# First of four images: normalisation moved from the pixels into the projection weights, and its front reordered

## The chip, the cores and the metric

One core of a Trainium2 chip runs the whole program. The metric is device time in microseconds (us) of one execution. TensorE (PE) multiplies matrices and writes PSUM; VectorE (DVE), ScalarE (ACT) and GpSimd (POOL) work element by element; SyncE (SP) issues the DMAs. Each engine works through its own instructions in the order in which they are written, and waits on semaphores that the others raise.

## The reference, cut to what matters

The input holds 4 images of 256 channels and 32 x 32 pixels, in float32.

```
gn(v):  per group of 8 channels: (v - mean) / sqrt(var + 1e-5)
x = x + concat(hifi, lofi)                        # 128 channels each, of gn(x)
  hifi: q, k, v = xw @ h_qkv_w                    # 4 heads of 32, windows of 2x2 pixels
        softmax(q k / sqrt(32)) v @ h_proj_w + h_proj_b
  lofi: q = xh @ l_q_w                            # every pixel
        k, v = mean over each 2x2 window @ l_kv_w # 256 pooled places
        softmax(q k / sqrt(32)) v @ l_proj_w + l_proj_b
x = x + conv3x3(relu(y * mask(y))) + bias,  y = gn(x)
```

The mask of a channel is found from its centre of mass. gn before a projection is one scale and one bias per channel and image: `gn(x) = s*x + t`.

## The kernel before, in words

Channels lie on the 128 partitions, in two tiles (`KT = 2`). Nearly every product is made in three float32r parts (`split_mm`, L1118: high by high, high by low, low by high), so each operand has a high part (a rounded copy) and a low part (what the rounding left). The six projections have names by their columns in the weights: WQ, WK, WV (window attention), WLQ, WLK, WLV (pooled attention).

An image passes through a *front* (projections, maxima of the pooled scores, window scores and their softmax) and a *rest* (exponentials, values, output projections); the convolution of the image before fills TensorE's waits. Image 0 has no convolution beside it. Its front runs like this. VectorE takes the statistics (`first_moments`, L652), TensorE averages them over groups (`group_means`, L1168) and warms up with four products of 384 columns (`keep_warm`, L1156), VectorE turns the averages into scale and bias (`normalisation`, L685). ScalarE and VectorE then both normalise the image (L455, L1093), VectorE forms the low part (L709), pools 2x2 windows (`pooling`, L712) and splits the pooled tile. TensorE does the projections WLQ, pooled WLK and WLV, WQ, WK, WV (`front`, L1263). ScalarE copies the queries' high part out of PSUM (L511), VectorE forms the low part (L840); then SyncE copies both within SBUF into the stacked operand `qs`, and the keys into `ks` (`stack`, L275): twelve copies, the first six of which release the first score block (semaphore `stacked`). Eight blocks of pooled scores follow (L1335), and VectorE takes the maxima of each (L851). The maxima are turned by TensorE (L1352), split by VectorE and copied into two more rows of `qs` (`stack_maxima`, L298), after which `pooled_scores` (L1234) can run. Beside this GpSimd multiplies queries by keys for the four places of a window (`products`, L377), TensorE sums them over each head (`window_scores_of`, L1252), ScalarE copies the sums (L594), TensorE transposes them (L1363), and VectorE does the window softmax (`window_maxima`, L863). TensorE turns the weights back (`turned_weights`, L1391), ScalarE copies them to `p_w` (L611).

In the rest, TensorE spreads the window weights (`values`, L1398) and VectorE multiplies them with the window values: four products into `pv` (L989). TensorE's pooled scores 5 to 7 stand behind `values(2)` and `values(3)`, which wait for the first and second of these products (L1417 to L1421). When all eight score tiles are through the exponentials (L566), TensorE sums them (`by_head`, L1242), projects the outputs, and goes on to image 1.

The convolution weights are also split on the way: VectorE makes two low parts (`first_weights`, L824, operations of L343) and three sums of taps (`turned_taps`, L830).

The order is written out by hand in every engine's block. PSUM has four tiles of two banks: `slot0` to `slot2`, and `cps`. In this file's lists `slot<-ks,qs` is a score block, `slot<-qs,ks` pooled scores, `cps<-mask,cst` and `cps<-probs,cst` window scores.

Of the kernel before, what the change touches and what calls it, by code (L numbers as in the profile page):

```python
# [5 lines left out]
F32 = mybir.dt.float32  # L6
# [7 lines left out]
P = 128  # L14
# [41 lines left out]
LA_SLOT = (0, 1, 2, 0, 1, 2, 0, 1)  # L56
ST_SLOT = (0, 1, 0, 1, 1, 0, 2, 1)
# [26 lines left out]
WARM = (4, 1)  # L84


PAIR_AFTER = (4, 7)
# [6 lines left out]
def pooled_by(images):  # L94


    return min(images, 1) + max(images - 2, 0)
# [21 lines left out]
def build(nc, x, wqkv, whp, wlp, bh, bl, cw, cb, mw, filt, consts, selectors, out):  # L119
    with ExitStack() as ctx:  # L120
# [34 lines left out]
        pv = (q_w[:], k_w[:], xn[:, 0], xn[:, 1])  # L155
# [5 lines left out]
        raw = probs[:, 2:4].rearrange("p a b -> p (a b)")  # L161
# [12 lines left out]
        pool_t, pool_s = mask[:, :, 0:2 * G], mask[:, :, 2 * G:3 * G]  # L174

# [7 lines left out]
        idle = sb("idle", [P, 1])  # L183

# [7 lines left out]
        cw_in, c_in, cst_in = sem("cw_in"), sem("c_in"), sem("cst_in")  # L192
        w_in = [sem(f"w_in{i}") for i in range(len(PIECES))]
        w_high, w_low, w_pooled = sem("w_high"), sem("w_low"), sem("w_low_pooled")
# [40 lines left out]
        def means_at(b, i):  # L235

            return (slot[1] if i == 0 else slot[2] if b else cps)[:, 0]
# [15 lines left out]
        def _(sp):  # L253
# [68 lines left out]
            for k in range(KT):  # L322
                sp.dma_start(raw_cw[:, k].rearrange("p r d c -> p (r d c)"), cw[k]).then_inc(cw_in, 16)
            stack(0)
            load(1)
            load(2)
            stack_maxima(0)
# [8 lines left out]
        def projection_low(engine, cols):  # L336

            return engine.tensor_tensor(w_lo[:, :, cols], raw_w[:, :, cols], w_hi[:, :, cols].bitcast(F32),
                                        ALU.subtract)

# [4 lines left out]
        def product(b, j):  # L345

            return mask[:, j] if b == 0 and j < 2 else qk[:, j]
# [14 lines left out]
        def _(pool):  # L362
# [7 lines left out]
            def mask_sum(b, pooled):  # L370

                pool.wait_ge(mask_c, (b + 1) * N_MASK)
                pool.wait_ge(pool_c, pooled_by(pooled) * N_POOL)
# [3 lines left out]
            def products(b):  # L377

                for j in range(NW):
                    if b == 0 and j == 2:  # L380
                        pool.wait_ge(proj_pe, 5)
# [32 lines left out]
            def step(b, first, last):  # L414
# [4 lines left out]
                if b == 1:  # L419
                    mask_sum(0, 2)  # L420
                    pool.wait_ge(v_dve, KT)
                    pool.wait_ge(lv_pe, 1)
# [3 lines left out]
                else:  # L426
# [3 lines left out]
                    nc.gpsimd.tensor_tensor(pv[0], pv[0], pv[1], ALU.add).then_inc(pv_pool, 1)  # L430
# [4 lines left out]
            pool.wait_ge(w_high, 1)  # L435
            projection_low(nc.gpsimd, PIECES[0]).then_inc(w_low, 1)
# [1107 lines left out]
```

## Time and profile before

| | |
|---|---|
| runs | 345.47, 345.17, 348.8 us; median 345.47 us |
| profiled execution | 345.89 us, of which 343.6 us are from the first to the last instruction |
| busy | PE 311.3 us (91%), DVE 270.2 us (79%), ACT 148.5 us (43%), POOL 82.9 us (24%) |
| PE busy in slices of 8.6 us, tenths, first ten | 1 8 8 9 9 6 8 9 9 9 |
| granted PE clock in the same slices, tenths | 9 9 6 9 9 8 9 9 9 9 |

The busy rows say which engine works most; the slices show that the first 60 us are the emptiest. What bounds a stretch is read from its waits: a timeline row ends with the idle time before it and, after `<-`, what ended that idle time.

### The profile page before, as it was taken

How to read it: one execution, taken by the hardware profiler on the slowest of the kernel's cores; microseconds unless marked ns; L12 is line 12 of the kernel's file. 1: busy time of each engine (PE TensorE's matmuls, PEld its weight loads, DVE VectorE, ACT ScalarE, POOL GpSimd, SP SyncE). 2: the span in 40 equal slices, each digit the busy share in tenths (PEclk: the TensorE clock that was granted, in tenths of full speed). 3: DMA queues.
4: the chain of work that ended last, by engine and by line, in shares of the span. 5: the costliest groups of instructions: out<-in, count | busy, mean ns of one | idle time of the engine just before them, and what ended most of it. 6: DMA issues, size and time to landing. Idle time of an engine off the chain costs nothing.

```text
span 343.6 us, 4160 instructions
## 1 busy us (share of the span) xinstructions
PE 311.3 (91%) x1566; PEld 220.8 (64%) x1566; DVE 270.2 (79%) x488; ACT 148.5 (43%) x189; POOL 82.9 (24%) x46
## 2 busy tenths in 40 slices
PE   1889968999979899999799999999799999999995
PEld 1477444277966653788477645888487737877884
DVE  4973969878998696979989877789887757897572
ACT  2533549572672644453058854450255424031300
POOL 2084912440454020005900200009600200202000
PEclk9969989999989999999999999999999999999999
DMA  7789500029500000198011100396001000001003
GB/s 274 284 105 142 228 5 0 2 38 128 66 0 4 2 1 2 27 126 137 6 61 61 64 0 0 50 132 114 4 0 63 0 0 32 31 0 63 0 0 122
DMA packets 12067, 20.38 MB, mean 59 GB/s; under 512 B 2064, under 2 KB 8080, under 8 KB 11792
## 3 DMA queue, kind: packets, MB, share of 16 engines
q1 hardware_dynamic: 12048, 20.13, 28.5%
q8 instruction: 12, 0.20, 0.2%
q14 instruction: 7, 0.06, 0.1%
HBM read 7.93 MB, written 4.19 MB: 35 GB/s over the span
## 4 chain that ended last, share of the span: by engine, by line
PE 55%; DVE 25%; ACT 8%; issue 6%; POOL 3%; DMA 2%; SPq 0%; DVEq 0%; POOLq 0%
PE slot L1116 28%; PE cps L1148 15%; PE slot L1192 7%; DVE l_max L851 5%; DVE mask L787 3%; PE cps L1192 2%; ACT probs L566 2%; POOL probs L382 2%; DVE v_lo L817 1%; DMA xy<-x 1%; PE slot L1394 1%; PE cps L1116 1%; ACT xn_hi L455 1%; ACT p_w L611 1%; DVE xn L743 1%
## 5 line engine op out<-in xcount | busy, mean ns | idle before, releaser
L1148 PE MATMUL cps<-v_hi,cw_hi 128*128 128x512 f32 (+1 forms) x144 | 57.6, 400 | 3.6 <-DVE v_lo L817 2.9
L1148 PE MATMUL cps<-v_hi,cw_lo 128*128 128x512 f32 (+1 forms) x144 | 58.4, 405 | 0.0
L1148 PE MATMUL cps<-v_lo,cw_hi 128*128 128x512 f32 (+1 forms) x144 | 56.5, 392 | 0.0
L382 POOL TENSOR_TENSOR probs<-q_w,k_w 128x1024 f32<-128x1024 f32 x14 | 32.9, 2378 | 78.9 <-DVE rw L780 71.8
L851 DVE TENSOR_REDUCE l_max<-slot 128x4 f32<-128x1024 f32 x32 | 37.0, 1218 | 6.3 <-PE slot L1116 6.3
L566 ACT ACTIVATE probs<-slot 128x1024 f32<-128x1024 f32 x32 | 31.2, 1021 | 13.9 <-PE slot L1116 13.6
L1148 PEld LDWEIGHTS cps<-v_hi,cw_hi 128*128 128x128 f32 x144 | 27.4, 191 | 12.5 <-issue 5.3
L1148 PEld LDWEIGHTS cps<-v_hi,cw_lo 128*128 128x128 f32 x144 | 27.4, 190 | 9.0 <-issue 4.0
L1148 PEld LDWEIGHTS cps<-v_lo,cw_hi 128*128 128x128 f32 x144 | 27.4, 190 | 5.3 <-issue 0.4
L365 POOL TENSOR_TENSOR mask<-rw 128x1024 f32<-128x1024 f32 x8 | 15.2, 1910 | 56.2 <-DVE rw L780 56.2
L1116 PE MATMUL slot<-xn_hi,w_hi 128*128 128x512 f32 (+1 forms) x68 | 28.0, 412 | 0.8 <-DVE xn_lo L709 0.8
L1116 PE MATMUL slot<-xn_hi,w_lo 128*128 128x512 f32 (+1 forms) x68 | 26.7, 392 | 0.0
L1116 PE MATMUL slot<-xn_lo,w_hi 128*128 128x512 f32 (+1 forms) x68 | 26.6, 391 | 0.0
L549 ACT ACTIVATE xn<-mask 128x1024 f32<-128x1024 f32 x8 | 8.5, 1061 | 39.0 <-DVE mask L787 39.0
L560 ACT ACTIVATE v_hi<-mask 128x1024 fp32r<-128x1024 f32 x16 | 16.8, 1058 | 18.0 <-DVE mask L809 10.6
L1116 PE MATMUL slot<-qs,ks 98*128 98x512 f32 x64 | 20.8, 419 | 2.0 <-DMA qs<-probs 2.0
L817 DVE SCALAR_TENSOR_TENSOR v_lo<-mask,v_hi 128x1024 fp32r<-128x1024 f32 x16 | 19.2, 1221 | 3.8 <-ACT v_hi L560 3.8
L1116 PE MATMUL slot<-probs,cst 128*32 128x512 f32 x176 | 21.4, 596 | 0.0
L1116 PEld LDWEIGHTS slot<-ks,qs 96*128 96x128 f32 x128 | 18.2, 194 | 4.3 <-DVE l_max L851 2.1
L430 POOL TENSOR_TENSOR q_w<-q_w,k_w 128x1024 f32<-128x1024 f32 x3 | 7.2, 2415 | 56.8 <-DVE k_w L989 56.8
L1116 PE MATMUL slot<-ks,qs 96*128 96x256 f32 x128 | 19.6, 290 | 1.2 <-DVE l_max L851 0.8
L535 ACT ACTIVATE xn<-xy,gn 128x1024 f32<-128x1024 f32 x8 | 9.6, 1240 | 17.2 <-DVE gn L682 17.2
(197 smaller groups left out, 627.7 us busy)
## 6 DMA issues: line engine op xcount, KB each, us to landing
xy<-x SPq DMA_DIRECT2D x8, 512.0 KB, 5.9
out<-xy SPq DMA_DIRECT2D x8, 512.0 KB, 2.6
qs<-probs SPq DMA_DIRECT2D x12, 256.0 KB, 5.8
qs<-probs SPq DMA_DIRECT2D x24, 128.0 KB, 8.2
raw_cw<-conv_w SPq DMA_DIRECT2D x2, 1152.0 KB, 7.2
ks<-probs SPq DMA_DIRECT2D x12, 128.0 KB, 6.9
probs<-h_qkv SPq DMA_DIRECT2D x2, 192.0 KB, 4.3
probs<-l_kv SPq DMA_DIRECT2D x2, 128.0 KB, 4.3
```

The costliest lines, as they stand in the source:

```text
L365: nc.gpsimd.tensor_tensor(mask[:, k].rearrange("p (h w) -> p h w", h=H), rw[:, k, 0].unsqueeze(2).to_broadcast([P, H, W]), rw[:, k, 1].uns ...
L382: nc.gpsimd.tensor_tensor(product(b, j).rearrange("p (n w) -> p n w", n=NW), q_w[:].rearrange("p (n w) -> p n w", n=NW), k_w[:, j * G:(j + ...
L535: nc.scalar.activation(xn[:, k], img(b, k), ACT.Identity, bias=gn[1][:, 6, k:k + 1], scale=gn[1][:, 5, k:k + 1]).then_inc(yn_ready, 1)
L549: nc.scalar.activation(xn[:, k], mask[:, k], ACT.Relu).then_inc(relu, 1)
L560: nc.scalar.activation(v_hi[:, k, 2 * phase:2 * phase + 2].rearrange("p a b -> p (a b)"), mask[:, k], ACT.Copy, scale=TILE_SCALE[phase]).t ...
L566: nc.scalar.activation(probs[:, i], flat[score_slot(b, i)], ACT.Exp, scale=SCALE / NW)\
L787: nc.vector.scalar_tensor_tensor(mask[:, k], mask[:, k], -1.0, xn[:, k], ALU.max, ALU.mult).then_inc(masked, 1)
L817: nc.vector.scalar_tensor_tensor(v_lo[:, k, part].rearrange("p a b -> p (a b)"), mask[:, k], TILE_SCALE[phase], v_hi[:, k, part].rearrange ...
L851: nc.vector.tensor_reduce(l_max[:, bass.ds(n, HEADS, step=NB)], flat[LA_SLOT[n]].rearrange("p (h m) -> p h m", h=HEADS), AX_X, ALU.max, ne ...
L1116: return nc.tensor.matmul(dst, lhsT, rhs, start=start, stop=stop)
L1148: ins = nc.tensor.matmul(cps[:, pos % 2, y0 * WT:y1 * WT], (cw_hi, cw_hi, cw_lo)[part][:, k, pos, dy + 1, o * P:(o + 1) * P], (v_hi, v_lo, ...
L1192: ins = nc.tensor.matmul(last_bank(o, pos)[:, y0 * WT:y1 * WT], (cw_hi, cw_hi, cw_lo)[part][:, k, pos, dy + 1, o * P:(o + 1) * P], (v_hi, ...
```

## The change

For image 0 alone, the scale is multiplied into the projection weights instead of the pixels, and the bias becomes a shift of each projection's result (a product of the raw weights with the bias, added when a result is copied out of PSUM; the shifts of the values are carried into the output bias). The raw image is split into high and low part, the high one while the statistics run. The pooled keys and values are no longer projected from a pooled tile but summed by TensorE over the four places of a window (24 products of 256 columns for the keys, 48 of 128 columns for the values, where there were 6 and 12). Afterwards the plain weights are split again for the images 1 to 3. The raw weights now lie in the place of image 2, whose load therefore comes later. The front of image 0 has an order of its own on each engine; the normalisation of image 1 moves forward on VectorE, in front of the convolution weights. The diff, cut to its core:

```diff
-WARM = (4, 1)
-PAIR_AFTER = (4, 7)
+WARM = (3, 1)
+LA_SLOT_0 = (0, 1) * 4
+FIRST_KEYS, FIRST_VALUES = (4, 4, 4, 0, 0, 0, 0, 0), (0, 0, 0, 4, 4, 4, 0, 0)
...
+            load_taps(1)
             stack(0)
             load(1)
+            load_taps(0)
+            stack_maxima(0)
+            sp.wait_ge(w_high, len(PIECES) + 1)
...
             load(2)
-            stack_maxima(0)
...
             def inner_weights():
                 t = taps[1]
+                pool.wait_ge(gn_c[0], 2 * N_GN)
                 link(nc.gpsimd.tensor_tensor(t[:, 0], t[:, 0], t[:, 2], ALU.add), 5)
...
+            def first_step():
+                input_high()
+                scaled_weights()
+                first_projections()
...
+                input_moments(1, 0)
+                act.wait_ge(lv_pe, 1)
+                values_of(slot[2])
...
+                plain_weights()
+                act.wait_ge(ssum_pe, 1)
+                nc.scalar.copy(q_w[:], flat_cps).then_inc(ssum_sb, 1)
+                act.wait_ge(cw_in[0], 16)
+                weight_high(0, V_LEFT, 0)
+                weight_high(0, V_RIGHT, 2)
...
+            def first_front():
+                normalisation(0, 0)
+                dve.wait_ge(gn_c[0], N_GN)
+                input_low(0)
+                scaled_weights(0)
+                input_low(1)
+                scaled_weights(1)
+                scaled_weights(2)
+                query_lo(0)
+                key_lo(0)
+                dve.wait_ge(zeroed, 1)
+                maxima(0, range(NB))
+                maxima_parts(0)
...
+                plain_weights()
+                first_bias()
...
+                window_maxima(0)()
+                normalisation(1, 0)
+                first_weights(weights)
+                turned_taps(weights)
...
+                pe.wait_ge(shift_act, 2)
+                keys, vals = Projection(cps, WK), Projection(slot[2], WV)
+                for n in range(NB):
+                    keys.more(FIRST_KEYS[n])
+                    if n == NB - NW - 1:
+                        pe.wait_ge(qkv_sb, 1)
+                    vals.more(FIRST_VALUES[n])
+                    if n == 0:
+                        pe.wait_ge(stacked, STACK)
+                        pe.wait_ge(lq_dve, 1)
+                    elif n == 1:
+                        pe.wait_ge(lk_act, 1)
+                        pe.wait_ge(lk_dve, 1)
+                    else:
+                        pe.wait_ge(la_max, n - 1)
...
+                    for h in range(HEADS):
+                        ins = mm(flat[LA_SLOT_0[n]][:, h * G:(h + 1) * G], qs[0:SC, h, n * P:(n + 1) * P], ks[0:SC, h],
+                                 True, True)
+                    ins.then_inc(la_pe, 1)
+                pe.wait_ge(qkv_sb, 3)
+                pe.wait_ge(w_in[1], KT * 16)
+                shift_of(WV, slot[2][:, 1, AT_SHIFT + S_V:AT_SHIFT + S_V + 1])
+                shift_of(WLV, slot[2][:, 1, AT_SHIFT + S_LV:AT_SHIFT + S_LV + 1])
+                values_of_sums(slot[2])
+                window_scores_of(0, (0, 1), cps)
+                pe.wait_ge(zeroed, 1)
+                pe.wait_ge(la_max, NB)
+                nc.tensor.transpose(slot[2][:, 0, 0:P], l_max[:], cst[:, C_ID:C_ID + P]).then_inc(lmt_pe, 1)
+                window_scores_of(0, (2, 3), cps)
```

TensorE, from the projection of the window values to the turn of the maxima, before (`cps<-xn_hi,w_lo` is the last product of that projection):

```order
L1116 MATMUL cps<-xn_hi,w_lo 128x512
L1116 MATMUL slot<-ks,qs 128x256 [waits qkv_sb,stacked]
L1116 MATMUL slot<-ks,qs 128x256 [waits lk_dve,lk_act]
L1116 MATMUL slot<-ks,qs 128x256 [waits la_max]
L1116 MATMUL slot<-ks,qs 128x256 [waits third_stacked,la_max]
L1116 MATMUL cps<-mask,cst 32x512 [waits prod_ready,qkv_sb]
L1116 MATMUL slot<-ks,qs 128x256 [waits fourth_stacked,la_max]
L1116 MATMUL cps<-probs,cst 32x512 [waits prod_ready,qkv_sb]
L1352 MATMUL slot<-cst,l_max 128x128 [waits la_max,zeroed]
```

The same place now (the key projection `cps<-xn_hi,w_hi` and value projection `slot<-xn_hi,w_hi` stand between the score blocks; `slot<-w_hi,xn_hi` is the first of the 48 products of the pooled values):

```order
L1233 MATMUL cps<-xn_hi,w_hi 128x512 [waits shift_act]
L1233 MATMUL slot<-ks,qs 128x256 [waits lq_dve,stacked]
L1233 MATMUL cps<-xn_lo,w_hi 128x512 x4
L1233 MATMUL slot<-ks,qs 128x256 [waits lk_dve,lk_act]
L1233 MATMUL slot<-xn_hi,w_hi 128x512 [waits qkv_sb]
L1233 MATMUL slot<-ks,qs 128x256 [waits fourth_stacked,la_max]
L1233 MATMUL slot<-gn,xy 128x1 [waits w_in1,qkv_sb]
L1233 MATMUL slot<-w_hi,xn_hi 128x128
L1233 MATMUL cps<-mask,cst 32x512 [waits prod_ready] x2
L1468 MATMUL slot<-cst,l_max 128x128 [waits la_max,zeroed]
L1233 MATMUL cps<-xn,cst 32x512 [waits prod_ready] x2
```

Eight products of the keys and all twelve of the values came ahead of the first score block and now stand behind its wait; the pooled values and both pairs of window scores follow the last block.

VectorE, from the end of the window softmax to the first product with the window values, before:

```order
L878 CAST k_w<-k_w 128x32x4 [waits soft_c]
L879 TENSOR_TENSOR k_w<-k_w 128x32x4 [waits soft_c]
L833 TENSOR_TENSOR raw_cw<-raw_cw 128x3x256
L834 TENSOR_TENSOR raw_cw<-raw_cw 128x3x256 [waits cw_dve]
L835 TENSOR_TENSOR raw_cw<-raw_cw 128x3x256 [waits cw_dve]
L989 TENSOR_TENSOR q_w<-slot,v_w 128x1024 [waits pb_pe]
```

The same place now (between L777 and L763 stand ten more small instructions of the normalisation of image 1):

```order
L994 TENSOR_TENSOR k_w<-k_w 128x32x4 [waits soft_c]
L777 COPY gn<-slot 128x4 [waits gn1_pe]
L763 SCALAR_TENSOR_TENSOR gn<-gn 128x2 [waits gn1_c]
L355 TENSOR_TENSOR cw_lo<-raw_cw,cw_hi 128x768 [waits cw_act]
L355 TENSOR_TENSOR cw_lo<-raw_cw,cw_hi 128x768 [waits cw_dve]
L943 TENSOR_TENSOR raw_cw<-raw_cw 128x3x256 [waits cw_dve]
L944 TENSOR_TENSOR raw_cw<-raw_cw 128x3x256 [waits cw_dve]
L945 TENSOR_TENSOR raw_cw<-raw_cw 128x3x256 [waits cw_dve]
L1127 TENSOR_TENSOR q_w<-slot,v_w 128x1024 [waits pb_pe]
```

The twelve instructions of the normalisation and the two low parts of convolution weights now stand between the softmax and the first window product; before, the low parts came ahead of the maxima and the normalisation after the window products.

## Rows read from the trace of the kernel before

**Rows 1.** The page's first line: span of the profiled execution.

```profile
span 343.6 us, 4160 instructions
```

**Rows 2.** TensorE's timeline: start, duration, line, operation, count, idle before it.

```profile
7.68 0.56 PE L1116 MATMUL slot<-mv,cst 128*128 128x4 f32 x2 [7.68 <-DVE mv L664]
8.11 5.04 PE L1116 MATMUL cps<-cst 128*128 128x384 f32 x8
...
14.49 0.39 PE L1116 MATMUL slot<-xn_hi,w_lo 128*128 128x512 f32 x1
14.72 0.39 PE L1116 MATMUL slot<-xn_hi,w_hi 128*128 128x512 f32 x1
...
18.89 0.48 PE L1116 MATMUL slot<-p_w,w_hi 128*128 128x256 f32 x2 [1.91 <-DVE w_lo L338]
```

**Rows 3.** SyncE's timeline: issues of the copies into the stacked operands, images 0 and 1.

```profile
18.05 2.39 SPq L278 DMA_DIRECT2D qs<-probs  x3
22.97 1.84 SPq L282 DMA_DIRECT2D ks<-probs  x3
...
74.55 1.93 SPq L278 DMA_DIRECT2D qs<-probs  x3
```

**Rows 4.** DMA issues at 24.3 to 24.8 us: KB, us to landing (image 0's sixth copy).

```profile
ks<-probs SPq DMA_DIRECT2D x1, 128.0 KB, 5.2
```

**Rows 5.** TensorE's timeline: score blocks, window scores, pooled scores, image 1's first block.

```profile
32.56 1.60 PE L1116 MATMUL slot<-ks,qs 96*128 96x256 f32 x12
...
36.40 1.91 PE L1116 MATMUL cps<-mask,cst 128*32 128x512 f32 x8
...
39.85 2.62 PE L1116 MATMUL cps<-probs,cst 128*32 128x512 f32 x8
...
46.63 1.97 PE L1116 MATMUL slot<-qs,ks 98*128 98x512 f32 x4 [1.96 <-DMA qs<-probs]
...
85.87 2.06 PE L1116 MATMUL slot<-ks,qs 96*128 96x256 f32 x12 [0.26 <-DMA ks<-probs]
```

**Rows 6.** Stretches: length, busy us by engine (PE, PEld, DVE, ACT, POOL), PE clock, DMA, GB/s.

```profile
12.60:16.00 3.40, 2.60 (x11) 1.73 (x10) 3.34 (x4) 1.74 (x3) 0.00 (x0) 1.00 0.97 407
19.40:26.20 6.80, 6.80 (x25) 6.01 (x24) 4.73 (x6) 0.75 (x3) 6.72 (x5) 0.50 1.10 141
46.70:50.10 3.40, 3.40 (x13) 2.91 (x13) 3.26 (x6) 1.94 (x2) 0.00 (x0) 0.50 0.01 2
70.00:343.60 273.60, 257.90 (x1327) 188.01 (x1325) 219.36 (x405) 112.41 (x143) 54.22 (x25) 0.99 0.23 42
87.76:93.07 5.31, 5.31 (x51) 5.31 (x49) 5.31 (x6) 2.24 (x4) 3.05 (x2) 1.00 0.50 58
```

**Rows 7.** Timelines of ScalarE and GpSimd: the queries' high part, a sum of taps.

```profile
17.02 1.01 ACT L511 CAST probs<-slot 128x1024 fp32r<-128x1024 f32 x1 [2.67 <-PE slot L1116]
...
40.48 1.80 POOL L404 TENSOR_TENSOR raw_cw<-raw_cw 128x768 f32<-128x768 f32 x1
```

**Rows 8.** VectorE's timeline, image 0, and image 1's normalisation.

```profile
23.60 3.70 DVE L343 TENSOR_TENSOR cw_lo<-raw_cw,cw_hi 128x768 fp32r<-128x768 f32 x2
33.31 9.19 DVE L851 TENSOR_REDUCE l_max<-slot 128x4 f32<-128x1024 f32 x8 [6.01 <-PE slot L1116]
...
47.15 0.29 DVE L879 TENSOR_TENSOR k_w<-k_w 128x128 f32<-128x128 f32 x1
...
49.33 0.96 DVE L835 TENSOR_TENSOR raw_cw<-raw_cw 128x768 f32<-128x768 f32 x1
...
52.16 1.22 DVE L989 TENSOR_TENSOR q_w<-slot,v_w 128x1024 f32<-128x1024 f32 x1 [1.86 <-PE slot L1116]
...
60.38 0.16 DVE L696 COPY gn<-slot 128x4 f32<-128x4 f32 x1
...
62.53 0.16 DVE L682 SCALAR_TENSOR_TENSOR gn<-gn 128x2 f32<-128x2 f32 x1
```

**Rows 9.** Chain of waits that ended last: start, us, what.

```profile
57.85 9.46 PE slot L1116 x70
```

More of the change, by code:

```diff
@@ L593, in step @@
                 act.wait_ge(ssum_pe, b + 1)
-                nc.scalar.copy(q_w[:], flat_cps if first else flat[0]).then_inc(ssum_sb, 1)
+                nc.scalar.copy(q_w[:], flat[0]).then_inc(ssum_sb, 1)
                 if b > 1:
@@ L900, in residual @@
                 dve.wait_ge(out_pe, b * 2 + k + 1)
-                last = nc.vector.scalar_tensor_tensor(img(b, k), flat[s], bias[:, k:k + 1], img(b, k), ALU.add, ALU.add)
+                if b == 0:
+                    dve.wait_ge(bias_first, 1)
+                add = bias[:, k:k + 1] if b else shift[:, S_OUT + k:S_OUT + k + 1]
+                last = nc.vector.scalar_tensor_tensor(img(b, k), flat[s], add, img(b, k), ALU.add, ALU.add)
                 last.then_inc(y_ready, 1)
@@ L1005, in step @@
                     conv_result(0, (V_LEFT,))
-                if not last:
+                if not last and not first:
                     normalisation(b + 1, 0)
@@ L1261, in window_scores_of, with __init__, more @@
                     ins.then_inc(ssum_pe, 1)
-            def front(b, conv, first=False):
+            class Projection:
+                def __init__(self, to, c0):
+                    self.to, self.c0, self.at = to, c0, 0
+                def more(self, n):
+                    for m in range(self.at, self.at + n):
+                        part, k, i = m // 4, m // 2 % 2, m % 2
+                        ins = mm(self.to[:, i], (w_hi, w_hi, w_lo)[part][:, k, self.c0:self.c0 + P],
+                                 (xn_hi, xn_lo, xn_hi)[part][:, k, halves(i)], m < 2, m >= 10)
+                        if m == 11:
+                            ins.then_inc(proj_pe, 1)
+                    self.at += n
@@ new lines, in shift_of, with first_keys @@
+            def shift_of(c0, to):
+                for k in range(KT):
+                    ins = mm(to, raw_w[:, k, c0:c0 + P], gn[0][:, 6, k:k + 1], k == 0, k == KT - 1)
+                return ins
+            def first_keys(parts):
+                for part in parts:
+                    for j in range(NW):
+                        for k in range(KT):
+                            ins = mm(slot[1][:, 0, 0:G], (w_hi, w_hi, w_lo)[part][:, k, WLK:WLK + P],
+                                     (xn_hi, xn_lo, xn_hi)[part][:, k, j * G:(j + 1) * G], part == j == k == 0,
+                                     part == 2 and j == NW - 1 and k == KT - 1)
+                return ins
@@ L1265, in front @@
+            def front(b, conv):
                 starting = b == 1
@@ L1374, in front @@
                     conv.more(EARLY)
-                elif not first:
+                else:
                     Convolution(b - 1).more(EARLY)
@@ L1455, in rest @@
                     window_out()
-                else:
+                elif not first:
                     group_means(b + 1, 0)
@@ L1488, in _ @@
             keep_warm(WARM[0])
[L1489 to L1492 removed]
+            first_front()
             run(step)
```

388 lines of the change are left out of this document (227 added, 161 removed).

## The prediction, made before the changed kernel was run

> **What bounds the kernel now.** I read the page first: its span is 343.6 us [rows 1]; with what lies around it the profiled execution took 345.89, 0.42 above the median of the runs, 345.47. All sums below are made against 345.89. Next the chain of waits: from 57.85 one unbroken piece of TensorE runs 9.46 us to the end of image 0's sums [rows 9]. So what matters ahead of it is when that piece may start, and the timelines give it backwards. Its last operands are exponentials whose scores 5 to 7 stand behind `values(2)` and `values(3)`, and those wait for VectorE's window products. The first of these starts at 52.16 [rows 8]. From there to 57.85 are 5.69 us. I take this distance over and ask when the first window product starts now; this is the hinge of the whole forecast.
>
> Before, three things lead up to it: the maxima (33.31, eight in 9.19, one each 1.15) [rows 8], the window scores (last pair ends at 39.85 + 2.62 = 42.47) [rows 5], and the softmax that follows these and ends at 47.15 + 0.29 = 47.44 [rows 8], 4.97 later. VectorE then makes sums of taps until 49.33 + 0.96 = 50.29 and sits idle 1.86 [rows 8].
>
> **Step 1: the start.** The warm-up has three products instead of four: it ends three quarters into its 5.04 us, at 8.11 + 3.7, near 11.9 [rows 2]. I give a shift (two products of one column, each two records) 0.4 from the two records of 0.2 at 7.68 to 8.11 [rows 2]. Then WLQ, twelve products of 512 columns at 14.72 - 14.49 = 0.23 [rows 2], with eight key products of 256 columns in between, each 0.12 (twelve in 1.60, less a tail of some 0.2) [rows 5]: 3.8 us, done near 16.6. The raw split, scaled weights and low parts are short operations on ScalarE and VectorE beside this stream, which start with the statistics or with the image; if the stream had to wait for one of them, everything below would be later by it. ScalarE copies the high part (1.01, before from 17.02 on [rows 7]) until 17.8, where the first stacked copy is issued; before it was 18.05 [rows 3]. Almost nothing is won here.
>
> **Step 2: the copies.** Before, the first of the six was issued at 18.05, the sixth at the end of its group, near 24.2 [rows 3], and landed 5.2 later [rows 4], at 29.4: 11.35 after the first. For image 1 the first was issued at 74.55 [rows 3] and TensorE, waiting for a key copy, started at 85.87 [rows 5]: 11.3 again. So the first block can start at 17.8 + 11.3 = 29.1. Before, TensorE reached it at 32.56 [rows 5], busy with projections: the wait was covered. Now it has, after 16.6, sixteen key products (1.9), a shift (0.4), WQ (2.8) and the first four products of WK (0.9): it is dry at 22.6 and stands still for 6.5 us. Eight products of WK and twelve of WV, ready all this time, are queued behind the wait.
>
> **Step 3: from the first block to the window scores.** Work in TensorE's queue at full clock: eight blocks of four at 0.12 (3.8), twenty products at 0.23 (4.7), two shifts (1.0), 48 products of 128 columns (5.3, [rows 6], 87.76 to 93.07), two pairs of window scores at 1.9 [rows 5], the turn of the maxima (0.2): 18.9. To this come 0.9 in which the last two blocks wait for maxima at 1.15 each, and the clock. After an idle 1.91 us [rows 2] the granted clock was 0.50, the lower of the two levels (1.2 and 2.4 GHz), from 19.4 to 26.2 [rows 6]; after 1.96 [rows 5] it was 0.50 from 46.7 to 50.1 [rows 6]. An idle 6.5 should do the same. Bounds for its cost: nothing if it stays up, 3.4 if it takes as long as the longer stretch; I take 2.5, between the 1.7 of the short stretch and the 3.4. The last pair ends at 29.1 + 18.9 + 0.9 + 2.5 = 51.4, against 42.47. Adding 4.97 the softmax ends at 56.4, against 47.44: **9.0 later**. GpSimd's four products can start when the keys are copied, near 35.5, and the second pair of scores needs the last of them near 49.5, so they hide if one takes under 3.5 (before, the second pair of scores followed the first by 39.85 - 36.40 = 3.45 [rows 5] with two products to wait for); so do the plain weights, split on ScalarE and VectorE while TensorE sums the values. Without their cover, two operations of 1536 columns would stand ahead of the softmax.
>
> **Step 4: VectorE after the softmax.** It now runs image 1's normalisation (60.38 to 62.53 + 0.16, 2.3), two low parts and the sums of taps (2.9 from 47.44 to 50.29) before the first window product. The low parts took 3.70 before [rows 8]. Their bounds: two operations of the size of a sum of taps, 1.9, and 3.7 as measured, when GpSimd worked at the same time. GpSimd's first sum of taps (1.80, [rows 7]) is now released by the same normalisation that frees VectorE, so they meet again; I take 3.7. The Trainium skill, SBUF — State Buffer, Who interferes with whom, says that a VectorE instruction with two SBUF inputs and a GpSimd one that reads SBUF exclude each other; by it the pair would cost 1.9 + 1.80, the same 3.7. Sum 9.0 with the gaps: the product starts at 56.4 + 9.0 = 65.4, against 52.16: **13.2 later**. The old idle 1.86 is gone, and the normalisation's old place, covered by TensorE's piece, gives nothing back.
>
> **Step 5: to the end of image 0.** The window weights are ready long before VectorE is, so TensorE idles about 5 us more ahead of `values(2)`. At the lower level the two values and two score tiles on the way cost double: I add 1.4, bounds 0 and 3.1 (another 1.7 if the long piece begins low too). One group mean, 0.3, leaves the piece at 57.85. Sum: 13.2 + 1.4 - 0.3 = 14.3, so **360.2 us**. From image 1 on the order is the old one, so the delay is carried to the end. The later load of image 2, the convolution weights on ScalarE, and GpSimd's share I cost at nothing: the image is needed a front later, the others are needed by the first convolution; if they came late, that would add.
>
> **Rivals.**
> - *The tail on VectorE is hidden.* If step 4 and 5 cost nothing (the low parts fit before the window weights come), only the 9.0 of the softmax counts: 345.89 + 9.0 - 0.3 = 354.6. For it: before, VectorE idled 1.86 there. Against: 9.0 of work stands in line where 4.7 was free.
> - *The copies land when TensorE gets there.* If copies within SBUF ran at the 407 GB/s of the weights' load [rows 6] instead of the 141 seen while they run, 1152 KB would take 2.8 and land near 23.1. No long wait, no low clock: last pair at 23.1 + 18.9 + 0.9 = 42.9, product at 42.9 + 4.97 + 9.0 = 56.9, 4.7 late: 350.3. Two images' copies with 11.3 speak against it. The Trainium skill, DMA: Bandwidth & Descriptors, Where 436 GB/s comes from, has the fabric's 435 as the limit for copies within SBUF; the trace does not agree, 141 is what moves.
> - *The delay is taken up behind.* TensorE is idle 273.6 - 257.9 = 15.7 us from 70 on [rows 6]. Were nearly all of that waits for things that image 0 does not delay, such as loads, the end would not move, and the shorter piece would leave 345.6: no slower. It decides from 14.3 of the 15.7. Against it: the late waits are for VectorE's and ScalarE's work on the images themselves.
> - *The early part wins and little is lost.* If TensorE reordered around the blocked score block, the last pair could come near 42 and only step 4 remain, about 350.
>
> **How the numbers follow.** Forecast 72%; hidden tail 12%; fast copies or reordering 6%; taken up behind 6%; something that makes it faster that I do not see 4%. The forecast's own range: 355 (clock stays up, low parts uncontended) to 364.5 (clock low through the blocks and the long piece). Taking in the hidden tail the range is 353.5 to 364.5. A change of 1% (3.5 us) is about what a measurement of this kernel can tell from none. Faster by over 1%: 0.04; within 1%: 0.06; slower by over 1%: 0.90.
>
> **What would show it.** The sixth copy's landing near 29 and TensorE's idle time before the first score block, ended by a DMA (step 2); a granted 0.50 after it; the 48 products between the last block and the window scores, and the softmax's end near 56 (step 3); two L343-like operations of together 3.7 and the first window product near 65, with no idle time of VectorE before it (step 4). Copies landing before 23, window scores done by 43, or VectorE idle before its first window product would make it wrong.

## The result and the profile after

The changed kernel takes 364.38 us (median; its four executions took from 363.0 to 365.93), the kernel before 345.32: a ratio of 1.0528, 95% interval 1.0442 to 1.0615. Slower, as forecast, and inside the range (353.5 to 364.5), but only 0.12 below its upper end: two of the four executions (365.61 and 365.93) lie above it, and the central 360.2 was 4.2 too low. A ratio leaves out executions over 1.5% above the fastest of their kernel, a median takes in all. The profiled execution took 365.93; its page's first line, against [rows 1]:

```profile
span 364.0 us, 4316 instructions
```

TensorE's timeline of the changed kernel (columns as in [rows 2]) answers to [rows 5]:

```profile
12.68 2.41 PE L1233 MATMUL slot<-xn_hi,w_hi 128*128 128x512 f32 x12
...
21.96 1.10 PE L1233 MATMUL cps<-xn_hi,w_hi 128*128 128x512 f32 x4
29.60 1.22 PE L1233 MATMUL slot<-ks,qs 96*128 96x256 f32 x4 [6.54 <-DMA ks<-probs]
...
40.58 0.74 PE L1233 MATMUL slot<-ks,qs 96*128 96x256 f32 x4 [0.67 <-DVE l_max L966]
41.15 0.95 PE L1233 MATMUL slot<-gn,xy 128*128 128x1 f32 x8
41.96 0.31 PE L1233 MATMUL slot<-w_hi,xn_hi 128*128 128x128 f32 x1
...
50.52 3.63 PE L1233 MATMUL cps<-mask,cst 128*32 128x512 f32 x8
...
54.40 1.91 PE L1233 MATMUL cps<-xn,cst 128*32 128x512 f32 x8
...
71.15 1.22 PE L1233 MATMUL slot<-p_w,sel 128*128 128x512 f32 x2 [5.34 <-DVE q_w L1127]
...
77.02 3.64 PE L1233 MATMUL slot<-probs,cst 128*32 128x512 f32 x32 [1.65 <-ACT probs L627]
```

Five things are to be seen. TensorE stands still 6.54 before the first score block, for a copy. The eight products of one column at 41.15 are the shifts of the values; behind them the 48 products of the pooled values run from 41.96 to 50.5, which is 8.5 for work that took 5.31 in [rows 6]. The first pair of window scores takes 3.63, the second 1.91. Before the third value product TensorE waits 5.34 for VectorE. And the sums start at 77.02; before, they started at 58.13, behind the group mean at 57.85 that opened the long piece [rows 9]:

```profile
58.13 3.64 PE L1116 MATMUL slot<-probs,cst 128*32 128x512 f32 x32
```

Stretches of the changed kernel's trace (columns as in [rows 6]; the clock is third from the right):

```profile
29.60:34.00 4.40, 4.40 (x15) 3.87 (x16) 1.80 (x2) 0.00 (x0) 0.00 (x0) 0.53 1.20 141
...
41.00:44.00 3.00, 3.00 (x29) 3.00 (x28) 1.78 (x2) 2.91 (x5) 3.00 (x2) 1.00 0.01 3
44.00:50.50 6.50, 6.50 (x32) 6.40 (x31) 0.00 (x0) 0.20 (x2) 1.15 (x1) 0.50 0.00 0
50.50:54.00 3.50, 3.50 (x9) 0.56 (x8) 0.00 (x0) 1.80 (x3) 0.00 (x0) 0.50 0.00 0
...
71.00:75.50 4.50, 4.21 (x10) 2.97 (x10) 3.80 (x5) 1.59 (x2) 2.71 (x2) 0.59 0.00 0
...
187.00:191.00 4.00, 3.78 (x15) 2.21 (x19) 3.44 (x5) 0.00 (x0) 3.77 (x3) 0.57 0.15 27
262.50:266.00 3.50, 3.50 (x17) 1.42 (x19) 1.93 (x3) 0.00 (x0) 2.86 (x2) 0.52 0.04 9
```

The lower level of the clock (0.50) holds from 44.0 to 54.0. It also holds for most of the stretches from 29.6, 71.0, 187 and 262.5 on. VectorE's timeline, from the end of the softmax to the first window product, answers to [rows 8]; GpSimd's timeline has a sum of taps beside it:

```profile
61.08 0.29 DVE L994 TENSOR_TENSOR k_w<-k_w 128x128 f32<-128x128 f32 x1
...
63.45 0.16 DVE L763 SCALAR_TENSOR_TENSOR gn<-gn 128x2 f32<-128x2 f32 x1
63.52 3.46 DVE L355 TENSOR_TENSOR cw_lo<-raw_cw,cw_hi 128x768 fp32r<-128x768 f32 x2
67.02 0.96 DVE L943 TENSOR_TENSOR raw_cw<-raw_cw 128x768 f32<-128x768 f32 x1
...
69.88 1.22 DVE L1127 TENSOR_TENSOR q_w<-slot,v_w 128x1024 f32<-128x1024 f32 x1
```

```profile
63.69 2.48 POOL L431 TENSOR_TENSOR raw_cw<-raw_cw 128x768 f32<-128x768 f32 x1 [18.54 <-DVE gn L763]
```

No idle time stands ahead of the first window product any more (1.86 in [rows 8]): VectorE is the one that is late.

### The profile page after: what moved, and what is told of

The parts are those of the page before. It is cut to its first block, busy times and chain, and to the rows that moved or that the text cites. A ratio compares the mean times of both kernels' runs of the same rounds, so it can differ in the third digit from the quotient of the medians.

```text
span 364.0 us, 4316 instructions
## 1 busy us (share of the span) xinstructions
PE 324.1 (89%) x1638; PEld 232.6 (64%) x1638; DVE 267.5 (74%) x489; ACT 150.4 (41%) x196; POOL 80.1 (22%) x44
## 4 chain that ended last, share of the span: by engine, by line
PE 61%; DVE 23%; ACT 6%; issue 5%; DMA 3%; SPq 1%; DVEq 0%
PE slot L1233 30%; PE cps L1265 16%; PE slot L1309 7%; DVE l_max L966 5%; PE cps L1233 4%; ACT probs L627 2%; PE cps L1309 2%; DMA ks<-probs 2%; DVE v_lo L927 1%; DVE mask L897 1%; DVE cw_lo L355 1%; DMA xy<-x 1%; DVE xy L1007 1%; DVE xn L853 1%; DVE st L739 1%
## 5 line engine op out<-in xcount | busy, mean ns | idle before, releaser
L1265 PE MATMUL cps<-v_hi,cw_hi 128*128 128x512 f32 (+1 forms) x144 | 58.6, 407 | 3.6 <-DVE v_lo L927 2.9
L1265 PE MATMUL cps<-v_hi,cw_lo 128*128 128x512 f32 (+1 forms) x144 | 59.3, 412 | 0.0
L1265 PE MATMUL cps<-v_lo,cw_hi 128*128 128x512 f32 (+1 forms) x144 | 57.4, 399 | 0.0
L408 POOL TENSOR_TENSOR probs<-q_w,k_w 128x1024 f32<-128x1024 f32 x12 | 28.2, 2384 | 78.9 <-DVE rw L890 71.8
L1233 PE MATMUL slot<-ks,qs 96*128 96x256 f32 x128 | 20.7, 295 | 7.6 <-DMA ks<-probs 6.8
L1233 PE MATMUL slot<-xn_hi,w_hi 128*128 128x512 f32 (+1 forms) x76 | 27.1, 393 | 0.0
L1233 PEld LDWEIGHTS slot<-ks,qs 96*128 96x128 f32 x128 | 19.1, 198 | 10.6 <-DMA ks<-probs 7.7
L1233 PE MATMUL slot<-xn_hi,w_lo 128*128 128x512 f32 (+1 forms) x76 | 25.7, 372 | 0.0
L1233 PE MATMUL slot<-xn_lo,w_hi 128*128 128x512 f32 (+1 forms) x76 | 25.4, 370 | 0.0
L621 ACT ACTIVATE v_hi<-mask 128x1024 fp32r<-128x1024 f32 x16 | 16.8, 1059 | 18.0 <-DVE mask L919 10.6
L1233 PE MATMUL slot<-probs,cst 128*32 128x512 f32 x176 | 22.5, 623 | 1.6 <-ACT probs L627 1.6
```

Of the source, the lines that this page charges most:

```text
L408: nc.gpsimd.tensor_tensor(product(b, j).rearrange("p (n w) -> p n w", n=NW), q_w[:].rearrange("p (n w) -> p n w", n=NW), k_w[:, j * G:(j + ...
L621: nc.scalar.activation(v_hi[:, k, 2 * phase:2 * phase + 2].rearrange("p a b -> p (a b)"), mask[:, k], ACT.Copy, scale=TILE_SCALE[phase]).t ...
L1233: return nc.tensor.matmul(dst, lhsT, rhs, start=start, stop=stop)
L1265: ins = nc.tensor.matmul(cps[:, pos % 2, y0 * WT:y1 * WT], (cw_hi, cw_hi, cw_lo)[part][:, k, pos, dy + 1, o * P:(o + 1) * P], (v_hi, v_lo, ...
```

## The experiments

Each was run beside the kernel before on its own chip, so ratios are compared, not microseconds; 0.01 is 3.5 us, and an expected time divided by 345.32 is an expected ratio. Positions come from each run's profiled execution. Edits are to the changed kernel, and experiment 3 holds those of 2.

**1. VectorE's tail off the path.**

```diff
                 input_moments(1, 0)
+                act.wait_ge(cw_in[0], 16)
+                weight_high(0, V_LEFT, 0)
+                weight_high(0, V_RIGHT, 2)
...
                 maxima(0, range(NB))
+                first_weights(weights)
+                turned_taps(weights)
                 maxima_parts(0)
...
                 normalisation(1, 0)
-                first_weights(weights)
-                turned_taps(weights)
```

> Moves one part: ScalarE's two high parts of convolution weights go ahead of its copy of the pooled values, VectorE's two low parts and three sums of taps go between the maxima and their split, where VectorE is idle 11.7 us. Image 1's normalisation stays behind the window softmax. Theory (step 4, this work stands on the path): the first window product starts near 64.4 instead of 69.9, TensorE's idle 5.3 us before the third value product are gone and with them its low clock after it: 357.5 to 359. Rival (the tail is covered by something else that ends as late): 363 to 364.4.

Measured: 358.64, ratio 1.0312 (1.0246 to 1.0379). VectorE's and TensorE's timelines:

```profile
45.28 1.95 DVE L355 TENSOR_TENSOR cw_lo<-raw_cw,cw_hi 128x768 fp32r<-128x768 f32 x2 [2.90 <-ACT cw_hi L549]
...
60.76 0.29 DVE L994 TENSOR_TENSOR k_w<-k_w 128x128 f32<-128x128 f32 x1
...
64.14 1.23 DVE L1127 TENSOR_TENSOR q_w<-slot,v_w 128x1024 f32<-128x1024 f32 x1 [0.86 <-PE slot L1233]
```

```profile
69.88 3.64 PE L1233 MATMUL slot<-probs,cst 128*32 128x512 f32 x32 [1.40 <-ACT probs L627]
```

The first window product starts 5.74 earlier, of which 0.32 is an earlier end of the softmax (61.05), and waits for TensorE again; the sums start 7.14 earlier. The normalisation, left in place, is hidden by the turn and copy of the window weights.

**2. The 48 products into the wait for the copies.**

```diff
+                shift_of(WV, slot[1][:, 1, AT_SHIFT + S_V:AT_SHIFT + S_V + 1])
+                shift_of(WLV, slot[1][:, 1, AT_SHIFT + S_LV:AT_SHIFT + S_LV + 1]).then_inc(shift_pe, 1)
+                values_of_sums(slot[1])
                 pe.wait_ge(shift_act, 2)
                 keys, vals = Projection(cps, WK), Projection(slot[2], WV)
...
-                shift_of(WV, slot[2][:, 1, AT_SHIFT + S_V:AT_SHIFT + S_V + 1])
-                shift_of(WLV, slot[2][:, 1, AT_SHIFT + S_LV:AT_SHIFT + S_LV + 1])
-                values_of_sums(slot[2])
```

> Moves the 48 products of the pooled values, with their shifts, into TensorE's wait for the stacked copies (into another bank). Theory (steps 2 and 3: TensorE stands idle 6.5 us with this work ready behind): the idle time before the first block falls under 1 us, the low clock after it is gone, the window scores end near 44 instead of 56.3, where GpSimd's products, started when the keys are copied near 33.5, end last (43.3): 352. If the 48 narrow products themselves lower the clock: it falls there too, from about 25 on, and the time is 355 to 357. Rival (the wait for the copies only becomes another wait, for maxima or copies): 360 or more.

Measured: 354.25, ratio 1.0168 (1.0105 to 1.0232). The timeline of TensorE, and the stretch of the 48 products:

```profile
29.43 0.74 PE L1233 MATMUL slot<-ks,qs 96*128 96x256 f32 x4 [0.30 <-DMA ks<-probs]
...
43.15 1.90 PE L1233 MATMUL cps<-xn,cst 128*32 128x512 f32 x6 [0.81 <-POOL xn L408]
```

```profile
22.60:28.00 5.40, 5.40 (x51) 5.40 (x50) 0.00 (x0) 0.50 (x1) 0.00 (x0) 1.00 1.14 130
```

The window scores end at 45.05 instead of 56.31, 11.3 earlier, and GpSimd's products end last, as expected. Here the 48 products do not lower the clock by themselves.

**3. Both**, with image 0's convolution weights loaded at the start and split in the same wait.

```diff
             load_taps(1)
+            load_taps(0)
             stack(0)
             load(1)
-            load_taps(0)
...
                 key_lo(0)
+                first_weights(weights)
+                turned_taps(weights)
                 dve.wait_ge(zeroed, 1)
```

> Both parts at once: the 48 products and their shifts in the wait for the stacked copies, and image 0's convolution weights off the path. Their load is issued at the start, ScalarE's high parts follow the queries' copy, VectorE's low parts and sums of taps lie in its wait for the first score block. Image 1's normalisation stays behind the window softmax. Theory (these two and the clock that they cost are the whole loss): softmax end near 50.1 as with the moved products alone, first window product 2.5 to 3.2 later (near 53), the long piece of sums near 59, against 58.13 before: 0.3% to 0.8% slower than before, with the two later stretches of low clock. Rival (a further 5 us or more of the loss lies elsewhere, in the copies or in the order of image 0's projections): the piece starts at 63 or later, over 1.5% slower.

Measured: 348.59, ratio 1.0018 (0.9987 to 1.0048): no difference from before that these runs can tell. VectorE's and TensorE's timelines:

```profile
54.49 1.23 DVE L1127 TENSOR_TENSOR q_w<-slot,v_w 128x1024 f32<-128x1024 f32 x1 [1.88 <-PE slot L1233]
```

```profile
60.23 3.64 PE L1233 MATMUL slot<-probs,cst 128*32 128x512 f32 x32 [1.40 <-ACT probs L633]
```

The sums start at 60.23, 16.8 earlier than in the changed kernel. A short low stretch (0.57 from 50.5 to 54.5) slowed TensorE ahead of the first window product, which came at 54.49 instead of 53. So these two places, with the clock that they cost, are 16.8 of the 18.9 by which the sums came late; the 2.1 that are left in this trace would be 0.6%, where the interval of the ratio ends at 0.48%.

**4. Keys and values ahead of the first block.**

```diff
-FIRST_KEYS, FIRST_VALUES = (4, 4, 4, 0, 0, 0, 0, 0), (0, 0, 0, 4, 4, 4, 0, 0)
+FIRST_KEYS, FIRST_VALUES = (12, 0, 0, 0, 0, 0, 0, 0), (12, 0, 0, 0, 0, 0, 0, 0)
```

> Undoes one part of the change: all twelve products of the keys and all twelve of the values stand ahead of the first score block again, the rest of the changed kernel stays. Theory (they were queued behind the wait for the stacked copies, steps 2 and 3): the idle 6.5 us before the first block fall to about 2; the blocks then follow the maxima, 1.23 each, and the last block ends near 39.6 instead of 41.2. If the clock still falls during the 48 products of the pooled values, the gain is only these 1.6: 362.8. If it stays up, another 5: 357.8. Rival (the blocks wait for the maxima anyway, the interleaving costs nothing): 364.4, unchanged.

Measured: 366.04, ratio 1.0537 (1.0454 to 1.0621): no gain that can be told. TensorE's timeline and two stretches:

```profile
29.46 1.65 PE L1233 MATMUL slot<-ks,qs 96*128 96x256 f32 x8 [1.86 <-DMA ks<-probs]
...
36.73 2.35 PE L1233 MATMUL slot<-ks,qs 96*128 96x256 f32 x8 [0.19 <-DVE l_max L966]
...
54.44 1.91 PE L1233 MATMUL cps<-xn,cst 128*32 128x512 f32 x8
```

```profile
37.00:40.00 3.00, 3.00 (x14) 2.79 (x15) 2.82 (x3) 2.76 (x7) 0.00 (x0) 0.50 0.83 343
...
44.00:46.00 2.00, 2.00 (x11) 2.00 (x11) 0.00 (x0) 0.00 (x0) 0.00 (x0) 0.50 0.00 0
```

The wait fell to 1.86, and the last block ended at 39.08 instead of 41.32, 2.2 earlier (1.6 expected). But the clock fell at 30.0, half a microsecond behind this wait of 1.86, as it did behind those of 1.91 and 1.96 in [rows 2] and [rows 5], and it stayed low until 53.9, through the blocks and all 48 products: the window scores end at 56.35. In the changed kernel it came back at 33.8, among key products. So the products between the blocks may be worth the clock, which neither theory had; no run varies this alone.

**5. What makes the clock fall at 44.** First the eight one-column products alone are moved into the wait, out of the place just ahead of the 48.

```diff
+                shift_of(WV, slot[1][:, 1, AT_SHIFT + S_V:AT_SHIFT + S_V + 1])
+                shift_of(WLV, slot[1][:, 1, AT_SHIFT + S_LV:AT_SHIFT + S_LV + 1]).then_inc(shift_pe, 1)
                 pe.wait_ge(shift_act, 2)
...
-                shift_of(WV, slot[2][:, 1, AT_SHIFT + S_V:AT_SHIFT + S_V + 1])
-                shift_of(WLV, slot[2][:, 1, AT_SHIFT + S_LV:AT_SHIFT + S_LV + 1])
                 values_of_sums(slot[2])
```

> Moves only the eight products of one column (the shifts of the values) from just ahead of the 48 products of the pooled values into TensorE's wait for the stacked copies. Theory 1 of the clock (the thin stretch of one-column products and the short wait just ahead made the clock fall at 44): the 48 products and the window scores run at granted 1.00, 0.8 + 5.0 us less: 358.6. Theory 2 (the 48 products themselves, or something earlier, make it fall): it falls again within the 48 products and only 0.8 is gained: 363.6.

Measured: 362.2, ratio 1.0401 (1.0339 to 1.0462).

```profile
40.60:46.20 5.60, 5.60 (x52) 5.55 (x50) 1.85 (x2) 3.17 (x6) 4.22 (x2) 1.00 0.00 2
...
57.60:66.00 8.40, 4.73 (x10) 3.31 (x11) 8.26 (x7) 2.93 (x3) 4.46 (x3) 0.50 0.00 0
```

The 48 products keep 1.00, and the window scores end at 48.32 + 1.91 = 50.23, 6.1 earlier: theory 1, whose 358.6 is a ratio of 1.0385. A part is given back: the clock falls at 57.2 instead and is low through the values and into the long piece. Then the same with eight such products also left ahead of the 48:

```diff
+                for c0, at in ((WV, S_V), (WLV, S_LV)):
+                    shift_of(c0, slot[2][:, 1, AT_SHIFT + at:AT_SHIFT + at + 1])
                 values_of_sums(slot[2])
```

> Control for the clock: as the run that moved the eight one-column products into the wait for the copies, but eight one-column products (the same ones again, their results unused) also stand just ahead of the 48 products of the pooled values. Theory 1 (this thin stretch made the clock fall at 44): granted 0.50 again within the 48 products, window scores end near 55 to 56. Theory 2 (the shorter wait for the copies kept the clock up, 5.7 instead of 6.5 us): the 48 products stay at 1.00 and the window scores end near 51.

Measured: one execution of 367.42. The clock fell again, at 41.7, within the one-column products and ahead of the 48; the window scores end at 57.8. That spoke for theory 1. The next run spoke against it.

**6. The later copies held back.**

```diff
+                if b == 0:
+                    sp.wait_ge(stacked, 6 * 16)
                 for quarter, done in zip((2, 3), stacked_late):
```

> SyncE issues the six later stacked copies of image 0 only when the first six have landed; nothing else changes. Theory (the twelve copies share what moves, 141 GB/s; the first six are slowed by those issued behind them): the first block starts 1 to 2 us earlier, near 28. Rival (copies are served in the order of issue): the first block stays near 29.5, and the fifth block, which needs the later ones, waits: these 768 KB take 5.4 at 141 GB/s, so it starts near 37 to 38 instead of 36.

Measured: one execution of 362.62. TensorE's timeline, and the stretch that was low in the changed kernel:

```profile
29.52 1.22 PE L1235 MATMUL slot<-ks,qs 96*128 96x256 f32 x4 [6.26 <-DMA ks<-probs]
...
37.22 0.63 PE L1235 MATMUL slot<-ks,qs 96*128 96x256 f32 x4
...
41.15 0.95 PE L1235 MATMUL slot<-gn,xy 128*128 128x1 f32 x8
```

```profile
44.00:50.50 6.50, 6.50 (x47) 4.22 (x48) 0.81 (x4) 2.01 (x5) 1.16 (x1) 1.00 0.00 0
```

The first block starts where it did, with the first copy issued at 18.33 instead of 18.14. So those issued behind slow the first six by some 0.3 at most, and nearly all of the 11.4 us from the first issue to the sixth landing (18.14 to 29.56 in the changed kernel) are their own. The fifth block, at 37.22, did not wait either. But the clock stayed at 1.00 with the one-column products in their old place; it fell at 57.8 instead. The last block (40.58) and these products (41.15) start exactly where they do in the changed kernel, so neither the thin stretch nor its time within the execution decides alone.

**7. The changed kernel once more**, unedited, for a second profiled execution.

> The changed kernel itself once more, for a second profiled execution of the same program, since two kernels with the same thin stretch ahead of the 48 products kept and lost the clock there. Theory 1 (the stretch decides): granted 0.50 from about 44 to 54 again. Theory 2 (when the clock falls differs from one execution to the next; what is fixed is about how much is lost in all): the 48 products run at 1.00 in this execution and the low stretch lies elsewhere before 76, with about 12 us of lost clock up to there either way. Time: 4.5% to 6% over before.

Measured: 365.89, ratio 1.0522 (1.046 to 1.0584).

```profile
44.00:50.50 6.50, 6.50 (x33) 6.50 (x32) 0.00 (x0) 0.00 (x0) 0.32 (x1) 0.50 0.00 0
```

It fell again, at 41.4 and not at 44.0. The front ran 1.35 ahead here (first block at 28.25), but the point differs in the queue too: within the one-column products now, behind 18 of the 48 products then. So the same program loses the clock at somewhat different points, and this execution was low for longer (until 55.1; until 54.3 in the first). With the short wait and the one-column products ahead of the 48 it fell in four executions (two of this program, experiment 1 and the second of 5) and did not in one (6). Where dense work stood ahead it did not fall (2, 3), nor with the short wait alone (the first of 5). What tells the exception apart stays open.

**8. Versions that were to beat both.** Four were made, all with the folded weights, each on top of the one before; the diffs are cut to their core. The first stands on experiment 3:

```diff
-                first_keys((0,))
...
-                first_keys((1, 2)).then_inc(proj_pe, 1)
+                first_keys((0, 1, 2)).then_inc(proj_pe, 1)
...
+                keys.more(12)
...
+                values_of_sums(slot[1], (0,)).then_inc(half_pe, 1)
...
+                    if n == 4:
+                        window_scores_of(0, (0, 1), cps)
+                    elif n == 6:
+                        window_scores_of(0, (2, 3), cps)
...
                 ins.then_inc(stok_pe, 1)
+                values_of_sums(slot[2], (1,))
```

> A version that is to beat both: folded weights kept, front reordered once more. The queries' projection is finished before the pooled keys (copies issued about 1 us earlier, near 17); then queries and keys of the windows, and half of the 48 products, all ahead of the first block; the values between blocks 1 to 3, the window scores behind blocks 4 and 6, the other half of the products in the softmax's wait. Convolution weights of image 0 as in the run with both parts; image 1's normalisation and plain weights behind the window products. Theory (TensorE's queue order and VectorE's tail were the loss, not the fold): first block near 28.5, maxima end near 40, softmax ends near 43.5 to 45, the sums start near 53 to 55 against 58.13: 0.5% to 1.5% faster than before. Rival (the fold's own 54 more products and the low clock cost as much as they save): equal to before within 0.5%.

Measured: 348.59, ratio 1.004 (1.0006 to 1.0074).

```profile
20.00:57.00 37.00, 32.42 (x186) 23.99 (x184) 24.72 (x31) 18.25 (x27) 16.06 (x8) 1.00 0.50 77
```

```profile
57.25 5.34 PE L1239 MATMUL slot<-probs,cst 128*32 128x512 f32 x32
```

Here the clock stays up to the sums, and the first window product starts at 49.64, 2.5 earlier than before. Of this 0.9 is left at the sums, which start at 57.25 but take 5.34 instead of 3.64 at the lower clock (from 58.6 on); and VectorE's split of the plain weights (3.40) stands ahead of the product that ends the image. The second:

```diff
+                    nc.gpsimd.tensor_scalar(w_hi[:], raw_w, 1.0, 0.0, ALU.mult, ALU.add).then_inc(w_high, 1)
...
+                    if n >= 4:
+                        window_scores_of(0, (n - 4,), cps)
```

> The version that is to beat both, mended where its first trace showed new waits. GpSimd, idle there, splits the plain weights (VectorE's 3.4 us of it stood ahead of the product that ends image 0's output); one place's window scores follow each of the blocks 4 to 7 instead of two places behind two of them; ScalarE takes image 1's first statistics before the copy of the window scores; the window weights are turned before the first pooled scores, which wait for a DMA. Theory (these waits kept the folded front from paying): maxima end about 1 us earlier than the 41.5 of the first version, first window product near 47.5 to 48.5, sums start near 54.5 to 55.5 against 57.3, the product behind them another 1.8 earlier: 0.5% to 1.2% faster than before. Rival (whatever is won in image 0's front is spent in TensorE's low clock, as in the first version): within 0.4% of before.

Measured: 349.55, ratio 1.0062 (1.0029 to 1.0096): no better. One place's scores cost TensorE what a pair's did, so its maxima ended 1.0 later, at 42.6. The third and the fourth:

```diff
-                    if n >= 4:
-                        window_scores_of(0, (n - 4,), cps)
+                    if n == 6:
+                        window_scores_of(0, range(NW), cps)
```

> The second version with two changes. All four places' window scores (eight products) stand together behind block 6: the traces so far show 1.91 us for the two places of a pair and 1.90 for a single place, so pieces of one place doubled TensorE's time for them. And the two one-column products of the output's shift move from just ahead of the long piece of sums to just ahead of the turn of the maxima. Theory (products for different places, which write different 32 partitions, run side by side): the eight take about 2 us, not 4 or 7.6; maxima end near 40 instead of 42.6, softmax near 43.5 instead of 48.3, sums start near 53.5 to 54.5 against 58.13 before: 0.8% to 1.5% faster than before. Rival (they run one after another, the single place's 1.90 was a wait): the eight take 3.8, sums start near 56: within 0.5% of before.

Measured: 351.53, ratio 1.0048 (0.9999 to 1.0097). The twelve executions fall into two groups, four from 346.52 to 347.37 and eight from 350.86 to 352.61; the trace is of one of the slower and says nothing of the others. In it the places do run side by side, but the clock fell during them, and again from 42.5 to 53.5 (granted 0.53); the first window product came at 53.65.

```diff
+                    if n in (4, 5, 6):
+                        for _ in range(8 if n < 6 else 99):
+                            next(second, None)
+                window_scores_of(0, range(NW), cps)
-                values_of_sums(slot[2], (1,))
```

> Third version with one thing moved: the second half of the 48 products goes between the blocks 4 to 6, eight behind each, as cover for TensorE while it waits for maxima, and all four places' window scores follow block 7; its copy comes ahead of that of the window scores. Theory (in the third version the clock fell during the window scores at 36 and again from 42.5, and the second half, at half rate, held back the turned weights by 2.5 us; dense work between the blocks keeps the clock up): granted 1.00 from 28 to 41, softmax ends near 46, first window product near 48.5 to 49.5 instead of 53.7, sums start near 55 to 56.5: 0.3% to 1% faster than before. Rival (the clock falls in any case somewhere ahead of the long piece): sums start at 57.5 or later, within 0.4% of before.

Measured: 348.15, ratio 1.0036 (0.9998 to 1.0074): the rival. Its TensorE, and the stretch behind:

```profile
38.51 0.62 PE L1242 MATMUL cps<-mask,cst 128*32 128x512 f32 x2
38.52 0.62 PE L1242 MATMUL cps<-xn,cst 128*32 128x512 f32 x2
...
39.83 0.60 PE L1242 MATMUL cps<-xn,cst 128*32 128x512 f32 x2
...
58.09 5.17 PE L1242 MATMUL slot<-probs,cst 128*32 128x512 f32 x32
```

```profile
41.00:56.00 15.00, 10.11 (x41) 7.21 (x40) 8.98 (x16) 9.75 (x14) 4.91 (x3) 0.77 0.20 74
```

Up to 41 all is as planned: granted 1.00, softmax done near 46.8. Then TensorE has little to do, the clock falls, the turned weights and pooled scores take twice as long, and the sums start at 58.09, where they did before (58.13). No version beat the kernel before.

## Why the prediction was right, point by point

| | forecast | measured |
|---|---|---|
| first stacked copy issued | 17.8 | 18.14 |
| first score block | 29.1, after 6.5 idle | 29.60, after 6.54 |
| last window scores end | 51.4 | 56.31 |
| softmax ends | 56.4 | 61.37 |
| first window product | 65.4 | 69.88 |
| sums start (58.13 + 14.3) | 72.4 | 77.02 |
| profiled execution | 360.2 | 365.93 |

**Steps 1 and 2** held in their times. Step 1's own terms add up to 16.1 (11.9 + 0.4 + 3.8), not to the 16.6 that it states; measured, the shift took 0.7 (11.97 to 12.68) instead of 0.4, and ScalarE's copy started at 17.00. The earlier start that the fold could give did not come (18.14 against 18.05), and no run tries the fold in the old order. The chain of waits of the changed kernel has the copy on it (start, us, what):

```profile
21.49 8.07 DMA ks<-probs
```

Copies at the weights' rate, the second rival, are ruled out: the wait is there in every run that left it uncovered. (That rival's 23.1 is not worked out from its own terms either: 17.8 + 2.8 is 20.6.)

**Step 3** held in its queue and failed in its size: from first block to last window score 22.3 were forecast, and 26.7 came. The term is the clock. I took 2.5, with 3.4 as the upper bound, for one low stretch behind the idle 6.5. That stretch cost 4.40 x 0.47 = 2.1. I had not reckoned with a second, behind it in the same queue: 44.0 to 54.0 at half rate, 5.0. I priced the 48 products by a row in which they stand between dense work [rows 6]; here a short wait and one-column products stand ahead of them. The bound came from how long one stretch had lasted, and said nothing of how many there would be. That the median still lies in the range is in part luck: its upper end was meant for a low clock through the blocks and the long piece, but the blocks were back at 1.00 from 33.8 on and the long piece ran at 1.00.

**Step 4** held: 9.0 forecast, 69.88 - 61.37 = 8.5 measured, the two low parts 3.46 instead of 3.7, beside GpSimd's sum of 2.48. With GpSimd's sum out of the way, in experiment 1, they took 1.95. That experiment left 3.1 of the 8.5 (61.05 to 64.14); the rival of the hidden tail is thereby ruled out.

**Step 5**: from the first window product to the sums 7.0 forecast, 7.14 measured, with the idle 5.34 (about 5 forecast). What I had at nothing, the images behind, cost 1.5: from the sums to the end 364.0 - 77.02 = 286.98, before 343.6 - 58.13 = 285.47. The delay of 18.9 is 19.5 at the sums of image 2 and 20.3 at those of image 3, and ahead of each lies a low stretch, near 187 and 263. The same stretches of the kernel before:

```profile
168.10:172.10 4.00, 3.74 (x24) 1.85 (x25) 3.45 (x5) 0.00 (x0) 3.80 (x3) 1.00 0.12 29
243.60:247.10 3.50, 3.50 (x24) 1.58 (x23) 3.09 (x3) 0.19 (x1) 2.19 (x2) 1.00 0.04 9
```

The stream there is the same, earlier by 18.9, with the same waits ahead of it, and keeps 1.00. Nothing was taken up behind, the third rival: 77.02 - 58.13 = 18.9 is still there at the turn of image 1's maxima (123.48 against 104.59). Lateness does not explain the two stretches. The first version of experiment 8, whose sums start ahead of those of the kernel before, has both as well:

```profile
171.20:174.70 3.50, 3.50 (x16) 1.30 (x18) 3.38 (x3) 0.00 (x0) 2.74 (x2) 0.51 0.29 62
246.30:249.80 3.50, 3.50 (x18) 0.65 (x16) 2.79 (x3) 0.10 (x1) 2.28 (x2) 0.51 0.05 9
```

And the kernel before has a mean granted clock of 0.980 in the execution traced here, but anything from 0.961 to 0.985 in those beside experiment 3: how often its clock falls differs from one execution to the next. Whether the change brings these two stretches stays open.

The fourth rival, an early part that wins, did not come either; experiment 2 shows how much of it was to be had by covering the wait: the window scores end at 45.05, still 2.6 behind before.

## What to carry to other kernels

Work that is ready but queued behind a wait can be lost twice: for the wait itself, and for the clock, which here was low behind the idle time and, in most executions, once more behind a thin stretch. Price a moved operation at both levels of the clock, and count the stretches that could fall, not one. Operations "with time to spare" belong in a gap that the timeline shows (VectorE's 11 us before the first block), not behind the operation that ends a chain.

## What the runs showed of the hardware

Products that write different groups of 32 partitions run side by side: the eight for all four places took from 38.51 to 40.43, as long as the four of one pair (1.91) or the two of a single place (1.90). The Trainium skill, TensorEngine Tiling (Array Packing), Tiling Modes, says that tiles operate independently and in parallel; the trace agrees.

The clock falls at different points in executions of one program, at 44.0 and at 41.4. The Trainium skill, TensorE: Matmul & The Clock Gate, Part 1, has the activity monitor run freely, not reset when a kernel starts, and a change come at another point for it; the two executions agree, though none of these runs shows the monitor. Of the versions in experiment 8 the first two kept it up from the first block to the sums, and it fell within these, at 58.6 and 60.1; in the traces of the other two it fell before.
